# Layer 1 of a fused two-layer block: the chosen prototype weights are split and turned by DMA together with the weighed products, not on TensorE

## The chip, the cores and the metric

The kernel runs on one core of a Trainium2 chip. The metric is device time in microseconds of one execution, lower is better. Before the change three runs gave 3023.6 to 3030.8 us, with a median of 3023.89 us.

A core has TensorE (PE; its weight loads are listed as PEld), VectorE (DVE), ScalarE (ACT), GpSimd (POOL) and SyncE (SP), which here issues nearly all DMAs. Each has a queue of its own, works through it in order, and waits on semaphores.

## The reference, cut to what matters

Two layers work on `x` (64 sequences of 256 rows, 256 wide). Each adds a gated cross-attention over 77 context rows and then a gated feed-forward part. The part in question is the feed-forward of layer 1: each row chooses its two nearest of 32 prototypes and passes through their low-rank matrices, with weights that sum to 1.

```python
d2 = x2 + p2[None, :] - 2.0 * (xf @ prototypes.T)
dists = jnp.sqrt(jnp.maximum(d2, 0.0))
w = jax.nn.softmax(-dists / t, axis=1)
topw, topi = jax.lax.top_k(w, 2)
topw = topw / jnp.sum(topw, axis=1, keepdims=True)
for tslot in range(2):
    idx = topi[:, tslot]
    wt = topw[:, tslot:tslot + 1]
    h = jnp.einsum('nri,ni->nr', B[idx], xf)            # rank 16
    y = jnp.einsum('nor,nr->no', A[idx], h) + bias[idx]
    out = out + wt * y
x = x + jnp.tanh(g_ffn[1]) * out
```

The kernel computes all 32 x 16 = 512 low products of a row (`low`), multiplies them by the row's weights (`wsel`, 32 numbers, two of them not zero) and multiplies the result `hw` by the stacked up-matrices. The bias of the chosen prototypes is one more product, of `wsel` with the 32 x 256 table of biases.

## The kernel before

**Stages.** First come the keys and values and layer 0 (to about 1460 us of the profile). From there to the end runs `attention_ffn_phase`, layer 1, which the change touches. Its unit is a tile of 128 rows, 128 tiles in all. A body is one sequence, that is two tiles, h = 0 and h = 1. Bodies 0 to 15 and 48 to the end are written out, and bodies 16 to 47 are a loop of 16 bodies that runs twice.

**Pipeline.** A body works on many tiles at once: the scores of tile t, its softmax sums one tile later, its normalising two later, its turned probabilities and the product with the values three later (`attend`, L1465), the second layer norm (4), the low products (5), the choice of prototypes (6), the weighing (7), the up-product and the store (8). Nothing schedules this. The order of the code in each engine's `body` is the order in its queue, and semaphores tie the queues together.

**Exact products.** TensorE works on float16 pairs: a number is written as a high half and a low half, and `matmul3` (L150 to L152) adds hi x hi, hi x lo and lo x hi. The high half is always written by ACT with a copy; the low half is the difference from the original, on POOL or DVE.

**The weighed products.** `hw` (128 x 512) is made on POOL (`weigh`, L1199). ACT writes its high half (`weighed_high`, L1336) and POOL its low half (`weighed_low`, L1178) into `hw_parts`. A DMA transpose from SP (`turn_weighed`, L1095) turns the 1024 columns into `hwT`, eight blocks of 128 x 128. A tile later TensorE multiplies them by the up-matrices (12 products).

**The chosen weights.** DVE makes two rows of picks (L1658, two instructions a tile) and adds them into `wsel` (L1665). It writes the sum three times side by side, 96 columns, since the bias product wants hi, hi and lo rows. TensorE transposes `wsel` (L1502) into a PSUM bank, ACT copies 96 rows of it as float16 (`wselT`, L1384), and DVE subtracts to make the low half of the last 32 rows (L1638). The product of `wselT` with the three-part bias table (L1486) closes the up-product.

**Banks.** Five PSUM banks go round in a fixed order of uses (`Ring`). In a body the uses are, for h = 0: probT 0, probT 1, probT 2, ffn, low 0, low 1, wselT, out, q 0, q 1; for h = 1: probT 0, q 2, probT 1, probT 2, ffn, low 0, low 1, wselT, q 3, out. Each use waits until the use five places earlier has been read. So in h = 0 low 1 waits until DVE has read probT 0 (the first `a_probT_lo`, L1527), and `out` (attend) needs all three.

**POOL's order in a tile** (L1211 and on): in h = 0 first the low half of the normed rows (`rows_low`, L1168, one a body); then weigh (L1199), normalise (L1160, two pieces), the low half of `hw` (L1178), the choice's arithmetic (L1186 to L1192), the low half of the normed tile (L1173), and the softmax sums in three steps (L1148, L1150, L1151). A wait stands between the three steps, none between L1151 and the L1168 that follows it.

**DVE's order around the picks**: residual (L1604), statistics (L1645), weight (L1592, L1597: 128 x 1, two SBUF inputs), two picks (L1658), `wsel` (L1665), nearest prototypes (L1574, L1579), and with the next tile the row sums (L1539, L1541), three `a_probT_lo` (L1527) and the maxima.

Of the kernel before, what the change touches and what calls it, by code (L numbers as in the profile page):

```python
# [83 lines left out]
class Ring:  # L84
# [624 lines left out]
def attention_ffn_phase(nc, ctx, psum, const, src, src_rows, dst, keys, values, wq, score_scale, ffn, experts):  # L709
# [267 lines left out]
    def uses(i):  # L977

        names = []
        for h in range(TPB):  # L980
# [8 lines left out]
            names += of(7, [("wselT", h)])  # L989
# [6 lines left out]
    ring = Ring(uses, WORK, 0, END, BODIES)  # L996

    def freed(i, use):
# [11 lines left out]
        return (wselT_ready, t - 6) if what == "wselT" else (out_ready, t - 7)  # L1010
# [34 lines left out]
    def _(sp):  # L1045
# [45 lines left out]
        def turn_weighed(t, p):  # L1091
# [3 lines left out]
            sp.dma_start_transpose(hwT[p][:, :, :], flat(hw_parts[:, :, :])).then_inc(hwT_in[p], 16)  # L1095
# [41 lines left out]
    def _(pool):  # L1137
        pool.memset(wsel[:, :], 0.0).then_inc(wsel_zero, 1)
# [55 lines left out]
        def weigh(t, h):  # L1194
# [6 lines left out]
                               wsel[:, 0:NPROTO].unsqueeze(2).broadcast_to([P, NPROTO, RANK]), ALU.mult)\  # L1201
# [196 lines left out]
    def _(pe):  # L1398
# [67 lines left out]
        def body(i, u, j):  # L1466
            for h in range(TPB):
# [9 lines left out]
                if live(t - 8, NT):  # L1477
# [3 lines left out]
                    need(pe, wselT_ready, t - 7)  # L1481
# [4 lines left out]
                    filled(nc.tensor.matmul(bank[:, 0:D], wselT[:, :], ffn["bias"][:, :], start=False, stop=True),  # L1486
# [12 lines left out]
                if live(t - 7, NT):  # L1499
# [13 lines left out]
    def _(dve):  # L1513
# [94 lines left out]
        def body(i, u, j):  # L1608
            for h in range(TPB):
# [25 lines left out]
                if live(t - 7, NT):  # L1635
# [1393 lines left out]
```

## Time and profile before

| | before |
|---|---|
| median of three runs | 3023.89 us (3023.6 to 3030.8) |
| profiled execution | 3015.37 us |
| its span | 3013.7 us |
| PE busy | 2738.8 us (91%) |
| DVE busy | 2461.3 us (82%) |
| ACT busy | 2199.1 us (73%) |
| POOL busy | 2084.7 us (69%) |
| mean granted TensorE clock | 0.971 of full speed |

The profile is of one execution. Times in it are microseconds from the start of its span. The granted clock is full in all of layer 1 but its start, its end and some microseconds at 2205, where the loop ends one turn and begins the next. A body of layer 1 takes about 23.3 us in the loop and 23.15 us behind it.

### The profile page before, as it was taken

Reading aid. Unit: us, or ns where it says so; the run is one execution under the profiler, and the core shown is the slowest. Engines: PE = TensorE matmul, PEld = TensorE weight load, DVE = VectorE, ACT = ScalarE, POOL = GpSimd, SP = SyncE. Lnnn points to the kernel's source line nnn. Section 1 sums busy time; section 2 is a strip of 40 time slices with the busy share of each in tenths; the row PEclk is TensorE's granted clock in tenths of the full one; section 3 lists DMA queues with packets and bytes.
Section 4 is the critical chain, followed back from the end, with each engine's and each line's share of the span. In section 5 each row is a group of like instructions: output and inputs, shape, how many; then the busy total and the mean of one; then the engine's idle time right before and its main releaser. Section 6 shows DMA issues by size and latency. Waiting matters only on the chain.

```text
span 3013.7 us, 96194 instructions
## 1 busy us (share of the span) xinstructions
PE 2738.8 (91%) x31534; PEld 2164.9 (72%) x31534; DVE 2461.3 (82%) x5870; ACT 2199.1 (73%) x5452; POOL 2084.7 (69%) x2777
## 2 busy tenths in 40 slices
PE   3889897899999999789799999999999999999996
PEld 2444444687778777657588888888888888888884
DVE  6787786688888888675589989888888888989884
ACT  2666666677777777575577777788877788778873
POOL 3893000576667666644378888888888888888886
PEclk7999999899999999999899999999999999999998
DMA  5997666223223223632467777677776777767763
GB/s 153 354 352 293 242 256 255 78 78 92 84 80 89 83 81 94 221 101 59 103 144 162 151 152 149 145 152 149 149 142 147 150 151 146 149 149 153 148 132 79
DMA packets 568793, 455.47 MB, mean 151 GB/s; under 512 B 383616, under 2 KB 527600, under 8 KB 555312
## 3 DMA queue, kind: packets, MB, share of 16 engines
q1 hardware_dynamic: 548144, 402.29, 53.2%
q0 software_dynamic: 7328, 23.40, 2.5%
q10 hardware_dynamic: 12960, 25.23, 2.3%
q8 instruction: 195, 3.19, 0.5%
q14 instruction: 166, 1.36, 0.2%
HBM read 235.08 MB, written 148.83 MB: 127 GB/s over the span
## 4 chain that ended last, share of the span: by engine, by line
PE 33%; DVE 10%; issue 4%; POOL 2%; DMA 1%; ACT 1%; SPq 0%; DVEq 0%; POOLq 0%; ACTq 0%
PE banks L150 10%; PE banks L152 9%; PE banks L151 9%; DVE a_pick L1658 2%; PE banks L1450 2%; DVE a_probT_lo L1527 2%; PE banks L1436 2%; DVE a_y L1604 1%; DVE a_rsum L1539 1%; DVE a_stats L1645 1%; DVE a_wtop L1597 1%; PE banks L1502 0%; DVE a_qT_lo L1525 0%; DVE a_smax L1546 0%; POOL a_pn L1160 0%
## 5 line engine op out<-in xcount | busy, mean ns | idle before, releaser
L383 POOL TENSOR_TENSOR a_probT_lo<-a_expT,a_probT_hi 128x512 f16<-128x512 f32 x256 | 291.5, 1160 | 218.4 <-ACT a_probT_hi L466 218.4
L459 ACT ACTIVATE a_expT<-banks,a_top,w_score_scale 128x512 f32<-128x512 f32 (+1 forms) x384 | 272.3, 709 | 152.4 <-PE banks L550 146.0
L1160 POOL TENSOR_TENSOR a_pn<-a_prob,a_rsum 128x1024 f32<-128x1024 f32 (+1 forms) x256 | 310.3, 1233 | 53.3 <-DVE a_rsum L1541 53.2
L1243 ACT ACTIVATE a_qT_hi<-banks 128x512 f16<-128x512 f32 x252 | 149.8, 595 | 210.1 <-PE banks L152 210.1
L150 PE MATMUL banks<-a_xnT,w_q_hi 128*128 128x256 f16 x1024 | 281.9, 275 | 15.8 <-DMA a_xnT<-a_xn_parts 13.9
L150 PE MATMUL banks<-a_vo_front,a_probT_hi 128*128 128x256 f16 x1024 | 279.5, 273 | 9.6 <-DVE a_probT_lo L1527 3.6
L151 PE MATMUL banks<-a_xnT,w_q_hi 128*128 128x256 f16 x1024 | 281.7, 275 | 0.0
L152 PE MATMUL banks<-a_xnT,w_q_lo 128*128 128x256 f16 x1024 | 281.5, 275 | 0.0
L152 PE MATMUL banks<-a_vo_front,a_probT_lo 128*128 128x256 f16 x1024 | 279.3, 273 | 0.0
L151 PE MATMUL banks<-a_vo_front,a_probT_hi 128*128 128x256 f16 x1024 | 279.3, 273 | 0.0
L1243 ACT ACTIVATE a_probT_hi<-banks 128x512 f16<-128x512 f32 (+1 forms) x384 | 193.8, 517 | 42.2 <-PE banks L1450 41.3
L1525 DVE TENSOR_TENSOR a_qT_lo<-banks,a_qT_hi 128x512 f16<-128x512 f32 x252 | 172.3, 684 | 45.5 <-ACT a_qT_hi L1243 40.7
L550 PE MATMUL banks<-ident,a_shifted 128*128 128x128 f32 (+1 forms) x1280 | 204.4, 284 | 5.3
L1527 DVE SCALAR_TENSOR_TENSOR a_probT_lo<-banks,a_probT_hi 128x512 f16<-128x512 f32 (+1 forms) x384 | 206.9, 581 | 0.3 <-ACT a_probT_hi L1243 0.3
L2397 DVE SCALAR_TENSOR_TENSOR kv_vo_out<-banks,kv_vo_out 128x512 f16<-128x512 f32 (+1 forms) x312 | 191.6, 679 | 16.5 <-ACT kv_vo_out L2295 16.5
L1450 PE MATMUL banks<-ident,a_pn 128*128 128x128 f32 (+1 forms) x1280 | 197.6, 278 | 2.0 <-issue 2.0
L659 DVE TENSOR_TENSOR a_shifted<-banks,a_smax 128x1024 f32<-128x1024 f32 (+1 forms) x256 | 192.2, 793 | 3.8
L2295 ACT ACTIVATE kv_vo_out<-banks 128x512 f16<-128x512 f32 (+1 forms) x312 | 172.4, 603 | 29.4 <-DMA vo<-kv_vo_out 22.1
L150 PE MATMUL banks<-w_downT_hi,a_ynT 128*128 128x288 f16 (+1 forms) x512 | 145.0, 283 | 47.5 <-DVE a_probT_lo L1527 45.1
L1199 POOL TENSOR_TENSOR a_hw<-a_low,a_wsel 128x512 f32<-128x512 f32 x128 | 135.4, 1058 | 72.7 <-DVE a_wsel L1665 72.7
L649 DVE TENSOR_REDUCE a_smax<-banks 128x16 f32<-128x1232 f32 x128 | 183.6, 1435 | 2.2 <-PE banks L536 1.9
L1278 ACT ACTIVATE a_prob<-banks,a_third_shift,w_score_scale 128x77 f32<-128x77 f32 x512 | 170.7, 414 | 12.0 <-ACT a_third_shift L1273 0.4
(383 smaller groups left out, 10315.9 us busy)
## 6 DMA issues: line engine op xcount, KB each, us to landing
vo<-kv_vo_out SPq DMA_DIRECT2D x38, 2048.0 KB, 7.8
a_vo_front<-vo SPq DMA_DIRECT2D x128, 512.0 KB
kt<-kv_k_out ACTq DMA_DIRECT2D x9, 2560.0 KB, 15.0
a_k<-kt SPq DMA_DIRECT2D x64, 308.0 KB, 3.4
kv_raw_e<-in_L_ffn_w POOLq DMA_DIRECT2D x16, 1024.0 KB, 8.8
a_x<-in_x SPq DMA_DIRECT2D x64, 256.0 KB, 2.9
a_y<-in_x SPq DMA_DIRECT2D x64, 256.0 KB, 2.7
x<-a_y SPq DMA_DIRECT2D x64, 256.0 KB, 2.8
```

The lines of the kernel that those rows point to most:

```text
L150: nc.tensor.matmul(out, lhs[0], rhs[0], start=start, stop=False)
L151: nc.tensor.matmul(out, lhs[0], rhs[1], start=False, stop=False)
L152: return nc.tensor.matmul(out, lhs[1], rhs[0], start=False, stop=stop)
L383: pool.tensor_tensor(probT[b][1][:, first:end, :], expT[b][:, first:end, :], probT[b][0][:, first:end, :], ALU.subtract).then_inc(prob_rea ...
L459: act.activation(expT[1 - h][0:rows, first:end, :], bank, ACT.Exp, bias=top[0:rows, 0:1], scale=weights["score_scale"][0:rows, 0:1]).then_ ...
L550: last = nc.tensor.transpose(bank[0:rows, c * P:(c + 1) * P], shifted[1 - h][:, place:place + rows], ident[:, :])
L659: last = nc.vector.tensor_tensor(shifted[h][:, cols].rearrange("p (r h k) -> p r h k", r=TILES, k=end - first), held_scores[:, :, :, first ...
L1160: last = pool.tensor_tensor(keys_of(pn[h]), e[:, :, first:end].rearrange("p (a c) k -> p a c k", a=outer), rsum[h][:, :].rearrange("p (a c ...
L1243: act.activation(out, bank[:, 0:cols].rearrange("p (c s) -> p c s", c=out.shape[1]), ACT.Copy, scale=scale)\
L1450: last = nc.tensor.transpose(bank[0:rows, c * P:(c + 1) * P], turned, ident[:, :])
L1527: nc.vector.scalar_tensor_tensor(out=lo, in0=bank, scalar=scale, in1=hi, op0=ALU.mult, op1=ALU.subtract)\
L2397: nc.vector.scalar_tensor_tensor(out=vo_out[q][0:m, placed(b), 1, :], in0=product_banks(g, c, b, m), scalar=1.0 / OUT_TOP, in1=vo_out[q][0 ...
```

## The change

Into one tile of 1152 columns, `hw_all`, go the 1024 columns of `hw_parts`, the 96 columns of `wsel_parts` (hi, hi, lo) and 32 columns of zeros. `wsel` shrinks to 32 columns.

```diff
-    wsel = sb("wsel", [P, P])
-    wselT = sb("wselT", [BIAS_ROWS, P], F16)
+    wsel = sb("wsel", [P, NPROTO])
-    hw_parts = sb("hw_parts", [P, 2, LOW], F16)
-    hwT = [sb(f"hwT{p}", [P, 2 * LC, P], F16) for p in range(2)]
+    TURNED = 2 * LC + 1
+    hw_all = sb("hw_all", [P, TURNED * P], F16)
+    hw_parts = hw_all[:, 0:2 * LOW].rearrange("p (s n) -> p s n", s=2)
+    wsel_parts = hw_all[:, 2 * LOW:2 * LOW + BIAS_ROWS].rearrange("p (r n) -> p r n", r=3)
+    hwT = [sb(f"hwT{p}", [P, TURNED, P], F16) for p in range(2)]
...
-            names += of(7, [("wselT", h)])
+            names += of(7, [("spare", h)])
...
-            sp.dma_start_transpose(hwT[p][:, :, :], flat(hw_parts[:, :, :])).then_inc(hwT_in[p], 16)
+            sp.dma_start_transpose(hwT[p][:, :, :], hw_all[:, :]).then_inc(hwT_in[p], 16)
...
+        sp.wait_ge(pad_zero, 1)
         load_x(2, 2, 0)
...
-        pool.memset(wsel[:, :], 0.0).then_inc(wsel_zero, 1)
+        pool.memset(hw_all[:, 2 * LOW + BIAS_ROWS:], 0.0).then_inc(pad_zero, 1)
...
             need(pool, hw_hi, t + 1)
+            pool.tensor_tensor(wsel_parts[:, 2, :], wsel[:, :], wsel_parts[:, 0, :], ALU.subtract)
             pool.tensor_tensor(hw_parts[:, 1, :], hw[:, :], hw_parts[:, 0, :], ALU.subtract).then_inc(hw_lo, 1)
...
+            act.activation(wsel_parts[:, 0:2, :], wsel[:, :].unsqueeze(1).broadcast_to([P, 2, NPROTO]), ACT.Copy)
             act.activation(hw_parts[:, 0, :], hw[:, :], ACT.Copy).then_inc(hw_hi, 1)
...
-                    act.activation(wselT[:, :], bank[0:BIAS_ROWS, 0:P], ACT.Copy).then_inc(wselT_hi, 1)
...
-                    need(pe, wselT_ready, t - 7)
...
-                    filled(nc.tensor.matmul(bank[:, 0:D], wselT[:, :], ffn["bias"][:, :], start=False, stop=True),
+                    filled(nc.tensor.matmul(bank[:, 0:D], hwT[turned][0:BIAS_ROWS, 2 * LC, :], ffn["bias"][:, :], start=False, stop=True),
...
-                    need(pe, wsel_ready, t - 6)
-                    bank = bank_for(i, ("wselT", h))
-                    filled(nc.tensor.transpose(bank[:, 0:P], wsel[:, :], ident[:, :]), i, ("wselT", h))
...
-                    nc.vector.tensor_tensor(wselT[rows, :], bank[rows, 0:P], wselT[rows, :], ALU.subtract)\
-                        .then_inc(wselT_ready, 1)
...
-                    need(dve, wselT_ready, t - 6)
-                    need(dve, hw_ready, t - 6)
-                    nc.vector.tensor_tensor(wsel[:, 0:BIAS_ROWS].rearrange("p (r n) -> p r n", r=3),
...
+                    need(dve, hw_lo, t - 6)
+                    nc.vector.tensor_tensor(wsel[:, :], pick[:, 0, :], pick[:, 1, :], ALU.add).then_inc(wsel_ready, 1)
```

The ring keeps an unused place, called `spare`, where `wselT` stood, so that no other use moves to another bank. Nobody fills or waits for it; the waits look one round further back. A bank now has its own number of fills in a body, so that the loop bodies hold some more register instructions on DVE and ACT.

Three places in the order of instructions, all in a late body, h = 1 first on POOL, which now splits the chosen weights ahead of the weighed products (`a_hw_all` is the new joint tile, `a_hw_parts` the old one). Before:

```order
L1199 TENSOR_TENSOR a_hw<-a_low,a_wsel 128x512
L1160 TENSOR_TENSOR a_pn<-a_prob,a_rsum 128x2x8x64
L1160 TENSOR_TENSOR a_pn<-a_prob,a_rsum 128x8x2x13
L1178 TENSOR_TENSOR a_hw_parts<-a_hw,a_hw_parts 128x512
L1186 TENSOR_TENSOR a_dist<-a_square,a_numbers 128x2
```

and now:

```order
L1208 TENSOR_TENSOR a_hw<-a_low,a_wsel 128x512
L1168 TENSOR_TENSOR a_pn<-a_prob,a_rsum 128x2x8x64
L1168 TENSOR_TENSOR a_pn<-a_prob,a_rsum 128x8x2x13
L1186 TENSOR_TENSOR a_hw_all<-a_wsel,a_hw_all 128x32
L1187 TENSOR_TENSOR a_hw_all<-a_hw,a_hw_all 128x512
L1195 TENSOR_TENSOR a_dist<-a_square,a_numbers 128x2
```

POOL has one instruction more in each tile. On ACT a copy moves from behind the low products to ahead of the high half of `hw`. Before:

```order
L1305 ACTIVATE a_inv<-a_rstd 128x1
L1336 ACTIVATE a_hw_parts<-a_hw 128x512
L1370 ACTIVATE a_yn<-a_y,a_shift,a_rstd 128x256
L1311 ACTIVATE a_ysq<-a_inv,a_mv 128x1
L1328 ACTIVATE a_yn_parts<-a_yn 128x256
L1381 ACTIVATE a_low<-banks 128x256 x2
L1384 ACTIVATE a_wselT<-banks 96x128
```

and now:

```order
L1314 ACTIVATE a_inv<-a_rstd 128x1
L1345 ACTIVATE a_hw_all<-a_wsel 128x64
L1346 ACTIVATE a_hw_all<-a_hw 128x512
L1380 ACTIVATE a_yn<-a_y,a_shift,a_rstd 128x256
L1320 ACTIVATE a_ysq<-a_inv,a_mv 128x1
L1337 ACTIVATE a_yn_parts<-a_yn 128x256
L1391 ACTIVATE a_low<-banks 128x256 x2
```

ACT has as many instructions as before. On TensorE the transpose between the low products and `attend` is gone. Before:

```order
L151 MATMUL banks<-w_downT_lo,a_ynT 128x256
L152 MATMUL banks<-w_downT_hi,a_ynT 128x256
L1502 MATMUL banks<-ident,a_wsel 128x128
L150 MATMUL banks<-a_vo_front,a_probT_hi 128x256
L151 MATMUL banks<-a_vo_front,a_probT_hi 128x256
```

and now:

```order
L157 MATMUL banks<-w_downT_lo,a_ynT 128x256
L158 MATMUL banks<-w_downT_hi,a_ynT 128x256
L156 MATMUL banks<-a_vo_front,a_probT_hi 128x256
L157 MATMUL banks<-a_vo_front,a_probT_hi 128x256
```

The bias product itself stays. DVE loses the subtraction for `wselT` (L1638).

## Rows read from the trace of the kernel before

**Rows 1.** Busy time by engine in the loop's stretch (windows; us and instructions).

```profile
1860.00:2580.00 720.00, 693.48 (x8464) 601.80 (x8463) 633.83 (x1810) 572.26 (x1719) 630.16 (x894) 1.00 0.72 148
```

**Rows 2.** What PE waited for, 1500 to 3000: total us, times, longest.

```profile
PE banks L150 <- DVE a_probT_lo L1527: 48.9, 63, 1.8
PE banks L150 <- DMA a_hwT<-a_hw_parts: 12.1, 5, 5.5
```

**Rows 3.** Timeline of DVE around one turn of a body: start, us, instruction, [idle before].

```profile
2696.68 0.48 DVE L1604 SCALAR_TENSOR_TENSOR a_y<-banks,out_scale,a_y 128x256 f32<-128x256 f32 x1 [1.39 <-PE banks L152]
...
2697.86 0.13 DVE L1597 TENSOR_TENSOR a_wtop<-a_late,a_wtop 128x1 f32<-128x1 f32 x1
2698.03 1.71 DVE L1658 TENSOR_SCALAR a_pick<-iota,a_topf,a_wtop 128x32 f32<-128x32 f32 x2
2699.77 0.26 DVE L1665 TENSOR_TENSOR a_wsel<-a_pick 128x96 f32<-128x96 f32 x1
...
2700.97 1.55 DVE L1527 SCALAR_TENSOR_TENSOR a_probT_lo<-banks,a_probT_hi 128x512 f16<-128x512 f32 x3
```

**Rows 4.** Timeline of POOL in the half body before and at that turn.

```profile
2691.93 1.16 POOL L1178 TENSOR_TENSOR a_hw_parts<-a_hw,a_hw_parts 128x512 f16<-128x512 f32 x1 [0.24 <-ACT a_hw_parts L1336]
...
2697.16 0.73 POOL L1150 TENSOR_TENSOR a_quarter<-a_half 128x256 f32<-128x256 f32 x1
2697.97 0.61 POOL L1151 TENSOR_TENSOR a_quarter<-a_quarter,a_prob 128x208 f32<-128x208 f32 x1
2698.54 1.16 POOL L1168 TENSOR_TENSOR a_xn_parts<-a_xn,a_xn_parts 128x512 f16<-128x512 f32 x1
2700.11 1.06 POOL L1199 TENSOR_TENSOR a_hw<-a_low,a_wsel 128x512 f32<-128x512 f32 x1 [0.41 <-DVE a_wsel L1665]
```

**Rows 5.** Chain that ended last, by line (page, whole span).

```profile
PE banks L150 10%; PE banks L152 9%; PE banks L151 9%; DVE a_pick L1658 2%; PE banks L1450 2%; DVE a_probT_lo L1527 2%; PE banks L1436 2%; DVE a_y L1604 1%; DVE a_rsum L1539 1%; DVE a_stats L1645 1%; DVE a_wtop L1597 1%; PE banks L1502 0%; DVE a_qT_lo L1525 0%; DVE a_smax L1546 0%; POOL a_pn L1160 0%
```

**Rows 6.** Timeline of ACT in h = 1 of the same body.

```profile
2689.16 0.38 ACT L1243 ACTIVATE a_probT_hi<-banks 104x256 f16<-104x256 f32 x1 [0.44 <-PE banks L1450]
...
2691.15 0.19 ACT L1305 ACTIVATE a_inv<-a_rstd 128x1 f32<-128x1 f32 x1
2691.24 0.62 ACT L1336 ACTIVATE a_hw_parts<-a_hw 128x512 f16<-128x512 f32 x1
```

**Rows 7.** Chain in order of time, same stretch: start, us on the chain, instruction.

```profile
2691.94 0.11 PE banks L1502
...
2700.97 0.64 DVE a_probT_lo L1527
2701.65 0.28 PE banks L150
...
2702.48 0.16 PE banks L1502
```

**Rows 8.** POOL's small and middle operations, whole run: ns min/median/max.

```profile
L1173 POOL TENSOR_TENSOR a_yn_parts<-a_yn,a_yn_parts x128: 667/670/675, 1506.5 to 2985.4; 128x256 f16<-128x256 f32 x128
...
L1186 POOL TENSOR_TENSOR a_dist<-a_square,a_numbers x128: 188/196/206, 1526.8 to 2996.9; 128x2 f32<-128x2 f32 x128
```

**Rows 9.** Timelines of DVE and POOL in body 8, where experts are added.

```profile
1663.35 1.31 DVE L1658 TENSOR_SCALAR a_pick<-iota,a_topf,a_wtop 128x32 f32<-128x32 f32 x2
...
1663.25 1.16 POOL L1168 TENSOR_TENSOR a_xn_parts<-a_xn,a_xn_parts 128x512 f16<-128x512 f32 x1
```

**Rows 10.** Timelines of DVE and POOL in an early h = 0.

```profile
1554.65 1.00 DVE L1658 TENSOR_SCALAR a_pick<-iota,a_topf,a_wtop 128x32 f32<-128x32 f32 x2
...
1554.68 0.73 POOL L1150 TENSOR_TENSOR a_quarter<-a_half 128x256 f32<-128x256 f32 x1
```

**Rows 11.** Landing of the hwT transpose (whole run), and its first reader in one body.

```profile
DMA to landing us min/median/max: 3.0/3.1/6.3
...
2698.72 0.27 PE L150 MATMUL banks<-w_upT_hi,a_hwT 128*128 128x256 f16 x1
```

**Rows 12.** The chain from 2915 us to the end, by line.

```profile
by line: issue 14.8%; POOL a_pn L1160 8.4%; POOL a_hw_parts L1178 8.0%; POOL a_hw L1199 7.5%; DMA a_hwT<-a_hw_parts 6.1%; POOL a_half L1148 5.1%; PE banks L150 4.8%; PE banks L152 4.4%; PE banks L151 4.2%; POOL a_dist L1189 4.1%; POOL a_lat
```

More of the change, by code:

```diff
@@ L84, with __init__ @@
 class Ring:
-    def __init__(self, uses, banks, first, last, steady):
-        self.banks, self.steady = banks, steady
+    def __init__(self, uses, banks, first, last, steady, spare=None):
+        self.banks, self.steady, self.spare = banks, steady, spare
         self.flat, self.at_use = [], {}
+        filled = [0] * banks
         for i in range(first, last):
             for name in uses(i):
-                self.at_use[i, name] = len(self.flat)
+                filled[len(self.flat) % banks] += name[0] != spare
+                self.at_use[i, name] = len(self.flat), filled[len(self.flat) % banks]
                 self.flat.append((i, name))
-        self.per = len(uses(steady))
-        assert self.per % banks == 0
+        kept = uses(steady)
+        assert len(kept) % banks == 0
+        start = self.at_use[steady, kept[0]][0]
+        self.per = [sum(name[0] != spare for name in kept[(s - start) % banks::banks]) for s in range(banks)]
         tails = [uses(i)[-banks:] for i in (steady - 1, steady)]
@@ L100, in fill @@
     def fill(self, i, name):
-        n = self.at_use[i if isinstance(i, int) else self.steady, name]
-        k = n // self.banks + 1
-        return n % self.banks, k if isinstance(i, int) else (i - self.steady) * (self.per // self.banks) + k
+        n, k = self.at_use[i if isinstance(i, int) else self.steady, name]
+        s = n % self.banks
+        return s, k if isinstance(i, int) else (i - self.steady) * self.per[s] + k
     def before(self, i, name):
-        n = self.at_use[i if isinstance(i, int) else self.steady, name] - self.banks
+        n = self.at_use[i if isinstance(i, int) else self.steady, name][0] - self.banks
+        while n >= 0 and self.flat[n][1][0] == self.spare:
+            n -= self.banks
         if n < 0:
@@ L799, in attention_ffn_phase @@
         sem("top_step"), sem("wtops_ready"), sem("picked"), sem("wsel_ready"))
-    low_ready, hw_ready, hw_hi, hw_lo, wselT_hi, wselT_ready, out_ready = (
-        sem("low_ready"), sem("hw_ready"), sem("hw_hi"), sem("hw_lo"), sem("wselT_hi"), sem("wselT_ready"),
-        sem("out_ready"))
+    low_ready, hw_ready, hw_hi, hw_lo, out_ready = (
+        sem("low_ready"), sem("hw_ready"), sem("hw_hi"), sem("hw_lo"), sem("out_ready"))
     minus_made = sem("minus_made")
@@ L1009, in freed @@
             return y_ready, t - 2
-        return (wselT_ready, t - 6) if what == "wselT" else (out_ready, t - 7)
+        return out_ready, t - 7
     def bodies(eng, body):
@@ L1200, in weigh @@
                                low[h][:, :].rearrange("p (n r) -> p n r", n=NPROTO),
-                               wsel[:, 0:NPROTO].unsqueeze(2).broadcast_to([P, NPROTO, RANK]), ALU.mult)\
+                               wsel[:, :].unsqueeze(2).broadcast_to([P, NPROTO, RANK]), ALU.mult)\
                 .then_inc(hw_ready, 1)
@@ L1381, in body @@
                         act.activation(low[1 - h][:, part], bank[:, 0:LOW // LU], ACT.Copy).then_inc(low_ready, 1)
-                if live(t - 7, NT):
-                    bank = full(i, ("wselT", h))
-                    act.activation(wselT[:, :], bank[0:BIAS_ROWS, 0:P], ACT.Copy).then_inc(wselT_hi, 1)
                 prep(4)
@@ L1634, in body @@
                     prototype_products(i, t - 5, h)
-                if live(t - 7, NT):
-                    bank, rows = full(i, ("wselT", h)), slice(2 * NPROTO, BIAS_ROWS)
-                    need(dve, wselT_hi, t - 6)
-                    nc.vector.tensor_tensor(wselT[rows, :], bank[rows, 0:P], wselT[rows, :], ALU.subtract)\
-                        .then_inc(wselT_ready, 1)
                 prep(4)
```

10 lines of the change are left out of this document (2 added, 8 removed).

## The prediction, made before the changed kernel was run

> **What bounds the kernel now.** I read the busy time first, then PE's waits, then the chain, then one turn of a body on each engine. Only layer 1 is touched, from about 1460 us on. In the loop's stretch of 720 us PE is busy 693.5, 96% [rows 1], so it looks like a kernel that TensorE bounds. But PE stands still about once a body, 48.9 us in 63 waits, and always for DVE's first `a_probT_lo` [rows 2]: low 1 needs the bank that it frees. So a loop through DVE sets the pace.
>
> Follow it back. `a_probT_lo` runs at 2700.97, behind the picks and `wsel` on DVE [rows 3]. The residual before them starts at 2696.68, as soon as PE has given it, and the last small weight (L1597) ends at 2697.99. Yet the two picks, 128 x 32 each, last 1.71 us, from 2698.03 to 2699.74, where `wsel` with 96 columns lasts 0.26; two like that would take 0.5 [rows 3]. POOL shows why: L1151 ends at 2698.58 and L1168 at 2699.70 [rows 4], and the second pick is done 0.04 us behind the latter. A pick that comes while POOL works is held until POOL's instruction ends, and since nothing stands between L1151 and L1168, the second pick is held for L1168 too. The chain charges 2% of the span, some 60 us, to L1658 [rows 5], about 1 us for each of 60 bodies.
>
> The Trainium skill (SBUF — State Buffer, "Who interferes with whom") has the reason: VectorE and GpSimd share one port pair, which `tensor_scalar` in its two-port mode holds exclusively, and the other fully blocks. By that rule, the trace agrees: both picks end with a POOL instruction.
>
> So what matters is when POOL ends L1168. POOL's queue is full back to L1178 at 2691.93, which waited 0.24 us for ACT [rows 4]. ACT's queue is full back to 2689.16, where it waited for PE's last turned probabilities in h = 1 [rows 6]. The loop is: PE turns probabilities in h = 1, ACT up to the high half of `hw` (ends 2691.86), POOL up to L1168 (2699.70), DVE up to `a_probT_lo` (2701.61), PE low 1 at 2701.65 [rows 7], `attend` of h = 0, and without a gap on to the next turning. PE's own way from that turning to the residual at 2696.68 reaches the picks 1.2 us too early: 2698.03 + 0.5 = 2698.5 for two picks that nothing holds, against 2699.74. Work taken from PE there is worth nothing; work put on ACT ahead of L1336 or on POOL between L1178 and L1168 is paid in full.
>
> **The change part by part**, per body, h = 1 unless said.
>
> ACT: the copy of 64 columns goes ahead of L1336, which is on the loop. A 128 x 1 lasts 0.19 and a 128 x 512 0.62 [rows 6], so 64 columns last about 0.19 + 0.43 x 63/511 = 0.24. The next instruction starts 0.10 before the end (2691.15 + 0.19 against 2691.24), so it costs 0.14; I take **+0.15**. Bounds: 0.09 (the step of the 128 x 1) and 0.52 (that of the 512). The copy L1384 that goes stood behind it and off the loop: nothing gained.
>
> POOL: the new 128 x 32 subtraction. A 128 x 2 lasts 0.196 and a 128 x 256 0.670 [rows 8]; between them 32 columns give 0.25. Neighbours overlap by 0.04 (2698.58 against 2698.54), so **+0.20**. Bounds 0.14 and 0.63. The 0.24 us that POOL waits before L1178 covers none of it, since the wait is for ACT and the new instruction waits for the same signal.
>
> DVE: `wsel` falls from 96 to 32 columns, between 0.26 [rows 3] and the 0.13 of a 128 x 1, about 0.17: **-0.09** on the loop, bounds 0 and -0.13. The subtraction L1638 goes, but DVE waits for PE anyway (1.39 us before L1604 [rows 3]): nothing. The new wait on `hw_lo` before `wsel` looks late: `hw_lo` of the tile before is signalled at 2691.93 + 1.16 = 2693.09, plus 0.35, and `wsel` runs at 2699.77. Over 6 us in hand; behind it in the queue would be row sums and `a_probT_lo`.
>
> PE, h = 0: the transpose took 0.16 of the chain at 2702.48 [rows 7], between low 1 and `attend`. But `attend` needs the third `a_probT_lo`, which ends at 2700.97 + 1.55 = 2702.52 [rows 3], and PE starts 0.04 after a release (2701.61 to 2701.65). So it may begin at 2702.56 to 2702.58 instead of 2702.64: **-0.06**, bounds 0 and -0.16.
>
> PE, h = 1: the transpose takes 0.11 [rows 7]. It only brings the residual 0.11 earlier to picks that are held: **0**, as above; -0.11 if the hold were gone.
>
> Sum: 0.15 + 0.20 - 0.09 - 0.06 = **+0.20 us a body**.
>
> Does the hold stay? POOL comes 0.35 later and DVE 0.11 earlier. L1150 then runs 2697.51 to 2698.24, and L1597 arrives at 2697.75: held until L1150 ends. The first pick comes 0.04 later, at 2698.28, and L1151 starts 0.08 after L1150 as now, at 2698.32. The trace has that very case: pick at 1554.65, POOL at 1554.68, and 1.00 us for the picks [rows 10], so a pick that comes 0.03 ahead is held all the same. It waits out L1151, and the second pick waits out L1168, to 2700.09. The pattern at the end is today's.
>
> That goes for some 46 bodies: +9.2 us. In the first dozen the experts are added and DVE runs later: the picks start at 1663.35, when L1168 (1663.25) already runs, so the first is held and the second ends 0.25 after L1168 (1664.66 against 1664.41) [rows 9]. With the shift of 0.46 it becomes the late pattern, which ends 0.04 behind L1168: 0.2 back, and nothing in sum.
>
> Tail: from 2915 us POOL leads the chain. 8.0% of 98.7 us are L1178 [rows 12], seven at 1.13 us each: 7 x 0.20 = 1.4. hwT has 6.1%, two landings of 3.0 us. The transpose carries nine blocks for eight; by size 3.1/8 = 0.39 at most and 0 at least, I take 0.17: 0.3. With ACT's 0.15 three times and `wsel`'s 0.09 three times back: **+1.9**. Start: SP waits for the memset before its first load, 0.1 us.
>
> DMA: hwT starts after 2693.1, lands 3.1 later, 2696.3, and is read at 2698.72 [rows 11]: 2.4 us in hand, 1.8 after the change. PE waited for it five times [rows 2]. Nothing.
>
> Total: 9.2 + 0 + 1.9 + 0.1 = +11.2. The profiled execution took 3015.4 (span 3013.7 and 1.7 around it): 3026.6. The median of the runs lies 8.5 above it, 3023.9: **3035**.
>
> **The rivals.**
>
> *PE bounds after all* (faster). For it: 96% busy, and every PE instruction but one wait a body on the chain. Then a body saves 0.11 + 0.06 + 0.09 = 0.26, over 60 bodies 15.6 us: 3009 or so. Against it: the end of the picks 0.04 behind L1168.
>
> *The picks slip into a gap* (faster). If ACT and POOL together cost over 0.55, L1150 starts after L1597 has passed; the first pick waits out L1150 only, the second takes the 0.08 us gap before L1151, and `wsel` waits out L1151 but not L1168. DVE would be 0.6 us earlier, and PE's wait of 0.77 a body (48.9/63) nearly goes: 46 x 0.65 = 30 us, about 2996. My terms give 0.35, their upper bounds more.
>
> *Who comes first gets the port.* The same section of the skill says that whoever issues first gets the pair. By that rule the pick at 2698.28 would go ahead of L1151 at 2698.32. Worked out from rows: the second pick waits out L1151 to 2698.97, and `wsel`, with two SBUF inputs, waits out L1168 to 2700.05 and ends 0.1 later, at 2700.16, where I expect 2700.09 + 0.17 = 2700.28 after the picks. That gives 0.1 a body back, +6 us in all: 3030. The early case speaks against it [rows 10].
>
> *The nine-block transpose is slow* (slower). Eight is a power of two and nine is not, and the trace shows no such transpose. At twice the landing (6.3, the row's maximum) hwT would come at 2699.9 for 2698.6, and `ynT` behind it later still, about 1 us a body: +60, 3085. Against it: the two sizes of transpose in use both work.
>
> *It comes out even*: ACT's and POOL's terms at their lower ends (0.23) against DVE's and PE's at their upper ones (0.29): 3024 to 3027.
>
> **How the numbers follow.** Below 0.3%, 9 us, a measurement can't tell a change from none. Forecast 0.54: its own range is +0.08 to +0.38 a body, 3029 to 3044; 0.44 of it is slower by more than 0.3%, 0.10 within. PE 0.12, gap 0.12, port rule 0.08, slow transpose 0.06, even 0.08. Faster 0.24, same 0.26, slower 0.50. The range leaves out the gap and the slow transpose: 3006 to 3046.
>
> **What would show it.** Right: PE's wait for `a_probT_lo` grows from 48.9 to about 70 us (0.20 + 0.11 + 0.05 more a body); the copy steps 0.15 and the subtraction 0.20; the picks still end 0.04 behind L1168 (now L1176); a body takes 23.35 late and 23.5 in the loop. Wrong: picks that end before L1168 does, a wait that shrinks, or PE waiting for hwT in mid-phase.

## The result, and the profile after

| | before | after |
|---|---|---|
| median of seven runs | 3023.60 us (3021.69 to 3030.80) | 3038.46 us (3035.11 to 3042.17) |
| ratio to before | | 1.0047, 95% interval 1.0035 to 1.0059 |
| profiled execution, its span | 3015.37, 3013.7 us | 3037.44, 3035.0 us |
| a body in the loop / behind it | 23.30 / 23.14 us | 23.64 / 23.45 us |

The change makes the kernel 0.47% slower, 14.9 us; the forecast was 3035 us, 11.2 us more. A body is read from one h = 0 residual to the next in DVE's timeline; the table has means.

The busy time in the loop's stretch, as in [rows 1]:

```profile
1860.00:2580.00 720.00, 675.84 (x8291) 583.68 (x8284) 621.75 (x1729) 567.50 (x1700) 636.43 (x938) 1.00 0.72 149
```

PE is busy 17.6 us less, DVE 12.1 less and ACT 4.8 less. POOL is busy 6.3 more, and the kernel is slower. The same 720 us now hold fewer bodies (23.64 us each for 23.30), so a part of each fall is only the slower pace: worked out per body, PE has 0.25 us less, DVE 0.10 less, ACT 0.11 more and POOL 0.50 more. What PE waited for in layer 1 (total us, times, longest) answers to [rows 2]:

```profile
PE banks L156 <- DVE a_probT_lo L1528: 77.4, 124, 1.8
PE banks L156 <- DMA a_ynT<-a_yn_parts: 6.5, 9, 2.0
PE banks L156 <- DMA a_hwT<-a_hw_all: 5.0, 4, 2.3
```

The wait for `a_probT_lo` has grown by 28.5 us and comes twice a body where it came once. DVE's timeline at the turn of a body behind the loop (start, us, instruction, [idle before]) answers to [rows 3]; its last row is the next body's residual:

```profile
2712.26 0.48 DVE L1605 SCALAR_TENSOR_TENSOR a_y<-banks,out_scale,a_y 128x256 f32<-128x256 f32 x1 [1.29 <-PE banks L158]
...
2713.43 0.54 DVE L1598 TENSOR_TENSOR a_wtop<-a_late,a_wtop 128x1 f32<-128x1 f32 x1
2714.01 1.80 DVE L1654 TENSOR_SCALAR a_pick<-iota,a_topf,a_wtop 128x32 f32<-128x32 f32 x2
2715.84 0.19 DVE L1660 TENSOR_TENSOR a_wsel<-a_pick 128x32 f32<-128x32 f32 x1
...
2716.97 1.55 DVE L1528 SCALAR_TENSOR_TENSOR a_probT_lo<-banks,a_probT_hi 128x512 f16<-128x512 f32 x3
...
2735.71 0.48 DVE L1605 SCALAR_TENSOR_TENSOR a_y<-banks,out_scale,a_y 128x256 f32<-128x256 f32 x1 [1.30 <-PE banks L158]
```

And POOL's, which answers to [rows 4]:

```profile
2707.77 0.25 POOL L1186 TENSOR_TENSOR a_hw_all<-a_wsel,a_hw_all 128x32 f16<-128x32 f32 x1 [0.65 <-ACT a_hw_all L1346]
2707.98 1.16 POOL L1187 TENSOR_TENSOR a_hw_all<-a_hw,a_hw_all 128x512 f16<-128x512 f32 x1
...
2713.22 0.74 POOL L1158 TENSOR_TENSOR a_quarter<-a_half 128x256 f32<-128x256 f32 x1
2714.03 0.61 POOL L1159 TENSOR_TENSOR a_quarter<-a_quarter,a_prob 128x208 f32<-128x208 f32 x1
2714.61 1.16 POOL L1176 TENSOR_TENSOR a_xn_parts<-a_xn,a_xn_parts 128x512 f16<-128x512 f32 x1
2716.11 1.06 POOL L1208 TENSOR_TENSOR a_hw<-a_low,a_wsel 128x512 f32<-128x512 f32 x1 [0.34 <-DVE a_wsel L1660]
```

The picture is that of before, moved. The body takes 2735.71 - 2712.26 = 23.45. L1598 ends at 2713.97, 0.01 behind L1158 (2713.96), where L1597 was held by nothing at the turn of [rows 3]; the prediction had that. The picks start 0.02 ahead of L1159 and end at 2715.81, 0.04 behind L1176 (2715.77). ACT's timeline in h = 1 answers to [rows 6]:

```profile
2704.85 0.39 ACT L1252 ACTIVATE a_probT_hi<-banks 104x256 f16<-104x256 f32 x1 [0.44 <-PE banks L1457]
...
2706.84 0.19 ACT L1314 ACTIVATE a_inv<-a_rstd 128x1 f32<-128x1 f32 x1
2706.93 0.25 ACT L1345 ACTIVATE a_hw_all<-a_wsel 128x64 f16<-128x64 f32 x1
2707.07 0.62 ACT L1346 ACTIVATE a_hw_all<-a_hw 128x512 f16<-128x512 f32 x1
```

The last fence of after is PE at that turn; it shows where the second wait of a body is:

```profile
2715.60 0.28 PE L1492 MATMUL banks<-w_low_bias,a_hwT 96*128 96x256 f16 x1
2716.36 0.30 PE L156 MATMUL banks<-w_downT_hi,a_ynT 128*128 128x288 f16 x1 [0.48 <-DMA a_ynT<-a_yn_parts]
...
2717.66 0.28 PE L156 MATMUL banks<-w_downT_hi,a_ynT 128*128 128x256 f16 x1 [0.39 <-DVE a_probT_lo L1528]
...
2718.67 0.27 PE L156 MATMUL banks<-a_vo_front,a_probT_hi 128*128 128x256 f16 x1 [0.19 <-DVE a_probT_lo L1528]
```

### The profile page after: what moved, and what is told of

It is laid out like the page before. It is cut to its first block, busy times and chain, and to the rows that moved or that the text cites. A ratio compares the mean times of both kernels' runs of the same rounds, so it can differ in the third digit from the quotient of the medians.

```text
span 3035.0 us, 95761 instructions
## 1 busy us (share of the span) xinstructions
PE 2724.8 (90%) x31406; PEld 2148.6 (71%) x31406; DVE 2442.4 (80%) x5742; ACT 2201.6 (73%) x5452; POOL 2114.3 (70%) x2905
## 4 chain that ended last, share of the span: by engine, by line
PE 34%; DVE 9%; issue 5%; POOL 2%; DMA 1%; ACT 1%; DVEq 0%; SPq 0%; POOLq 0%; ACTq 0%
PE banks L156 10%; PE banks L158 10%; PE banks L157 10%; PE banks L1457 2%; DVE a_pick L1654 2%; PE banks L1443 2%; DVE a_probT_lo L1528 2%; DVE a_wtop L1598 1%; DVE a_y L1605 1%; DVE a_stats L1641 1%; DVE a_rsum L1540 1%; POOL a_hw_all L1187 0%; POOL a_pn L1168 0%; DVEq L62 0%; DVE a_topi L1580 0%
## 5 line engine op out<-in xcount | busy, mean ns | idle before, releaser
L1168 POOL TENSOR_TENSOR a_pn<-a_prob,a_rsum 128x1024 f32<-128x1024 f32 (+1 forms) x256 | 310.6, 1235 | 51.7 <-DVE a_rsum L1542 51.5
L1156 POOL TENSOR_TENSOR a_half<-a_prob 128x512 f32<-128x512 f32 x128 | 166.5, 1301 | 14.1 <-ACT a_prob L1363 14.0
```

Source lines behind the costliest of these rows:

```text
L1168: last = pool.tensor_tensor(keys_of(pn[h]), e[:, :, first:end].rearrange("p (a c) k -> p a c k", a=outer), rsum[h][:, :].rearrange("p (a c ...
```

## Experiments

All were compared with the kernel before on the same chip. Bodies are means in us: the first dozen (read from bodies 3 to 12), the loop, behind it. Ratios have their 95% intervals.

| kernel | median, us | ratio to before | dozen | loop | behind |
|---|---|---|---|---|---|
| before | | 1 | 23.98 | 23.30 | 23.14 |
| after | 3038.46 | 1.0047 (1.0035 to 1.0059) | 23.95 | 23.64 | 23.45 |
| e1_swap | 3020.87 | 1.0016 (1.0002 to 1.0030) | 23.84 | 23.47 | 23.28 |
| e2_hidden | 3009.58 | 0.9981 (0.9969 to 0.9993) | 23.68 | 23.26 | 23.10 |
| e4_pool_op | 3027.24 | 1.0039 (1.0028 to 1.0051) | 23.90 | 23.51 | 23.35 |
| e6_nine_blocks | 3016.56 | 0.9999 (0.9989 to 1.0010) | 23.97 | 23.31 | 23.15 |
| e7_removed_only | 3012.49 | 0.9986 (0.9975 to 0.9996) | 23.92 | 23.26 | 23.12 |
| e11_even_after | 3036.01 | 1.0055 (1.0041 to 1.0069) | 23.93 | 23.65 | 23.45 |
| e3_rows_later | 3004.89 | 0.9957 (0.9940 to 0.9974) | 23.49 | 23.12 | 23.05 |
| e12_removed_rows_later | 3002.02 | 0.9956 (0.9942 to 0.9970) | 23.44 | 23.14 | 23.04 |
| e13_pool_op_rows_later | 3015.86 | 0.9994 (0.9984 to 1.0004) | 23.64 | 23.24 | 23.32 |
| e8_after_rows_later | 3019.19 | 1.0012 (1.0002 to 1.0021) | 23.54 | 23.48 | 23.13 |
| e9_hidden_rows_later | 3012.31 | 0.9990 (0.9978 to 1.0002) | 23.55 | 23.41 | 23.01 |
| e10_even_hidden_later | 3017.66 | 0.9987 (0.9977 to 0.9997) | 23.53 | 23.45 | 23.04 |

Medians are from different chips; compare the ratios.

### Where the additions stand

**e1_swap**: the weighed products first on both engines, the chosen weights behind them.

```diff
-            pool.tensor_tensor(wsel_parts[:, 2, :], wsel[:, :], wsel_parts[:, 0, :], ALU.subtract)
-            pool.tensor_tensor(hw_parts[:, 1, :], hw[:, :], hw_parts[:, 0, :], ALU.subtract).then_inc(hw_lo, 1)
+            pool.tensor_tensor(hw_parts[:, 1, :], hw[:, :], hw_parts[:, 0, :], ALU.subtract)
+            need(pool, wsel_hi, t + 1)
+            pool.tensor_tensor(wsel_parts[:, 2, :], wsel[:, :], wsel_parts[:, 0, :], ALU.subtract).then_inc(hw_lo, 1)
...
-            act.activation(wsel_parts[:, 0:2, :], wsel[:, :].unsqueeze(1).broadcast_to([P, 2, NPROTO]), ACT.Copy)
             act.activation(hw_parts[:, 0, :], hw[:, :], ACT.Copy).then_inc(hw_hi, 1)
+            act.activation(wsel_parts[:, 0:2, :], wsel[:, :].unsqueeze(1).broadcast_to([P, 2, NPROTO]), ACT.Copy)\
+                .then_inc(wsel_hi, 1)
```

> The changed kernel, with the order turned round on two engines: ACT copies hw first and the chosen weights behind it, POOL subtracts for hw first (on the signal of hw alone) and for the chosen weights behind it. Theory (the loop goes through ACT's high half of hw and POOL up to rows_low, with the picks held): ACT's 0.15 us leaves the loop, POOL's 0.20 stays in it, so a late body takes 23.30 us, against 23.45 in the changed kernel and 23.15 before; about 3031 us. Rival (the loss comes from something else that the change brings, the longer transpose or the register instructions): the body stays at 23.45 and the time at 3038.

A late body takes 23.28 (expected 23.30), and the ratio is 1.0016, where the expected 3031 us would be 1.0025, within the interval. ACT's copy was on the loop.

**e2_hidden**: both additions in a gap of their queue. `chosen_high` is ACT's copy with a signal of its own (`wsel_hi`); it now stands ahead of the third `a_probT_hi`.

```diff
+            need(pool, wsel_hi, t + 1)
+            pool.tensor_tensor(wsel_parts[:, 2, :], wsel[:, :], wsel_parts[:, 0, :], ALU.subtract)
             need(pool, hw_hi, t + 1)
-            pool.tensor_tensor(wsel_parts[:, 2, :], wsel[:, :], wsel_parts[:, 0, :], ALU.subtract)
             pool.tensor_tensor(hw_parts[:, 1, :], hw[:, :], hw_parts[:, 0, :], ALU.subtract).then_inc(hw_lo, 1)
...
+                    if g == PG - 1 and live(t - 7, NT):
+                        chosen_high(t - 7, u, h, j)
                     if live(t - 3, NT):
                         split_hi(i, ("probT", h, g), ...
```

> The changed kernel, with both additions put where their engines wait anyway: ACT's copy of the chosen weights ahead of the last turned probabilities (0.44 us idle there), POOL's subtraction ahead of its wait for the high half of hw (0.24 us idle). Theory: nothing is added to the loop, the shorter wsel takes 0.065 off it, a late body takes 23.09 to 23.12 us and PE waits for a_probT_lo 0.75 us in each; 3020 to 3025 us, level with before or a little below. Rival (transpose or registers): 23.45 and 3038, as in the changed kernel. Rival (PE bounds, its work was saved): 0.2 or more below before, 22.9 a body, 3010.

In e2 a stretch of ACT, then of POOL, from their timelines:

```profile
2685.74 0.25 ACT L1354 ACTIVATE a_hw_all<-a_wsel 128x64 f16<-128x64 f32 x1
2686.30 0.38 ACT L1253 ACTIVATE a_probT_hi<-banks 104x256 f16<-104x256 f32 x1 [0.30 <-PE banks L1468]
...
2688.37 0.62 ACT L1346 ACTIVATE a_hw_all<-a_hw 128x512 f16<-128x512 f32 x1
...
2688.52 0.24 POOL L1186 TENSOR_TENSOR a_hw_all<-a_wsel,a_hw_all 128x32 f16<-128x32 f32 x1
2689.06 1.16 POOL L1188 TENSOR_TENSOR a_hw_all<-a_hw,a_hw_all 128x512 f16<-128x512 f32 x1 [0.30 <-ACT a_hw_all L1346]
```

ACT waits 0.30 for PE where it waited 0.44, so the copy lies in that wait; POOL still waits 0.30 for ACT behind its subtraction. From ACT's last probabilities to the high half of `hw` it is 2.07 us, in the changed kernel 2.22 (2704.85 to 2707.07): ACT's 0.15 is gone. Behind the loop a body takes 23.10, as expected (23.09 to 23.12), and bodies 3 to 12 gain 0.30 each, which I had not worked out; so the ratio, 0.9981, is a little below the 0.9988 to 1.0005 of the expected times. The same work, moved, makes the kernel 0.66% faster than after (0.9981 by 1.0047) and a little faster than before. In e1 only the copy leaves the path, and a body is 0.17 shorter than in after. The place costs, not the work.

**e4_pool_op**: before, with one 128 x 32 subtraction more on POOL ahead of L1178.

```diff
+            pool.tensor_tensor(unused[:, :], hw[:, 0:NPROTO], hw_parts[:, 0, 0:NPROTO], ALU.subtract)
             pool.tensor_tensor(hw_parts[:, 1, :], hw[:, :], hw_parts[:, 0, :], ALU.subtract)
```

> The kernel before, with one more 128 x 32 subtraction on POOL behind its wait for the high half of hw, into a tile that nobody reads. Theory: 0.20 to 0.22 us more in each body, 23.36 late, and the picks end 0.04 behind rows_low as before; 3034 us. Rival (POOL's idle 0.24 us takes it up, or POOL is not on the loop): 23.15 and 3024.

Its two rows in POOL's timeline:

```profile
2721.95 0.24 POOL L1179 TENSOR_TENSOR a_unused<-a_hw,a_hw_parts 128x32 f16<-128x32 f32 x1 [0.45 <-ACT a_hw_parts L1338]
2722.15 1.16 POOL L1180 TENSOR_TENSOR a_hw_parts<-a_hw,a_hw_parts 128x512 f16<-128x512 f32 x1
```

A step of 0.20, and 0.21 more a body in the loop and behind it (expected 0.20 to 0.22): paid in full, although POOL waits 0.45 for ACT right ahead of it.

### What was removed, the transpose, the registers

**e7_removed_only**: after without its copy and its subtraction and with eight blocks turned; the bias product reads zeros, so the chosen biases are left out.

```diff
-            act.activation(wsel_parts[:, 0:2, :], wsel[:, :].unsqueeze(1).broadcast_to([P, 2, NPROTO]), ACT.Copy)
...
-            pool.tensor_tensor(wsel_parts[:, 2, :], wsel[:, :], wsel_parts[:, 0, :], ALU.subtract)
```

> The removals alone: TensorE's transpose, ACT's copy and DVE's subtraction are gone and wsel has 32 columns, but nothing is added to ACT, POOL or the DMA. The biases of the chosen prototypes are left out of the result (that product reads zeros). Theory: only wsel's 0.065 us is on the loop, a late body takes 23.08 us, low 1 to attend stays at 1.015 us although the transpose between them is gone, PE's wait grows by 0.05 to 0.1 a body; about 3020 us. Rival (PE's work counts): 0.26 less a body, 22.9, and 3008 us.

The rival in which PE bounds falls here: the means are 23.26 and 23.12, only 0.04 and 0.02 shorter, where that rival wanted 0.26 less a body. The median body behind the loop is 23.08, as expected, and low 1 to `attend` still takes 1.015. PE is rid of two transposes and waits the time away (stretch of layer 1):

```profile
PE banks L156 <- DVE a_probT_lo L1528: 58.5, 117, 1.7
```

That is 9.6 us more than before [rows 2].

**e6_nine_blocks**: before, turning nine blocks, the ninth all zeros.

```diff
...
-            sp.dma_start_transpose(hwT[p][:, :, :], flat(hw_parts[:, :, :]))
+            sp.dma_start_transpose(hwT[p][:, :, :], hw_all[:, :])
```

> The kernel before, with hwT's transpose alone enlarged from eight to nine blocks (the ninth holds zeros and nobody reads it); the chosen weights go their old way over TensorE. Theory: 23.15 us a late body as before, the transpose lands in 3.3 us for 3.1, PE waits for hwT only at the end; 3024 to 3026 us. Rival (the longer transpose costs part of the 15 us): PE waits for hwT or ynT in mid-phase, 0.1 us or more a body, 3029 or above.

Landing of that transpose, from issue, in e6:

```profile
DMA to landing us min/median/max: 3.2/3.4/5.9
```

It lands 0.3 later than with eight blocks [rows 11], and the time does not move.

**e11_even_after**: after, but the unused place of the ring counts as a fill, so that the loop has no more register instructions than before.

```diff
-                filled[len(self.flat) % banks] += name[0] != spare
+                filled[len(self.flat) % banks] += 1
...
+                            if n == LU - 1 and c == 0 and ("spare", h) in uses(i if isinstance(i, int) else BODIES):
+                                filled(last, i, ("spare", h))
                         filled(last, i, ("low", h, n))
```

> The changed kernel with the even count of fills alone, so without the extra register instructions in the loop. Theory (DVE's picks are held until POOL's L1176 ends, so that what DVE does ahead of them is free): no change, 23.61 us a body in the loop and 23.45 behind it, ratio to before 1.0047. Rival (the register instructions are part of what the change costs in the loop): the loop falls by 0.1 to 0.3 a body, 3 to 9 us in all.

Nothing moves: 23.65 and 23.45. The interval of the ratio (1.0041 to 1.0069) holds the expected 1.0047.

### The hold by `rows_low` taken away

**e3_rows_later**: before, with `rows_low` behind `weigh` in POOL's order. Nothing is added or removed.

```diff
-                if h == 0 and live(i + 1, NB):
-                    rows_low(i + 1)
                 if live(t - 7, NT):
                     weigh(t - 7, 1 - h)
+                if h == 0 and live(i + 1, NB):
+                    rows_low(i + 1)
```

> The kernel before, with POOL's rows_low (128 x 512, L1168) moved from ahead of weigh to behind it, so that in h = 1 to h = 0 nothing follows the last softmax sum but a wait for wsel. Theory (the picks are held by POOL's instructions): the second pick ends 0.04 us behind the last softmax sum and not behind rows_low, wsel comes about 1.1 us earlier, PE's wait of 0.77 us a body goes nearly or wholly, and PE's work or POOL's (21.3 us a body) bounds next: 22.3 to 22.8 us a body, 2980 to 3005 us. Rival (the picks are long for a reason of their own, POOL is a bystander): the picks still last 1.7 us, the body stays at 23.15 or grows, since xnT is turned later.

DVE, then POOL, at a turn of e3:

```profile
2689.55 0.45 DVE L1597 TENSOR_TENSOR a_wtop<-a_late,a_wtop 128x1 f32<-128x1 f32 x1
2690.04 0.51 DVE L1658 TENSOR_SCALAR a_pick<-iota,a_topf,a_wtop 128x32 f32<-128x32 f32 x2
2690.59 0.26 DVE L1665 TENSOR_TENSOR a_wsel<-a_pick 128x96 f32<-128x96 f32 x1
...
2689.38 0.61 POOL L1151 TENSOR_TENSOR a_quarter<-a_quarter,a_prob 128x208 f32<-128x208 f32 x1
2690.92 1.06 POOL L1199 TENSOR_TENSOR a_hw<-a_low,a_wsel 128x512 f32<-128x512 f32 x1 [0.93 <-DVE a_wsel L1665]
2691.94 1.16 POOL L1168 TENSOR_TENSOR a_xn_parts<-a_xn,a_xn_parts 128x512 f16<-128x512 f32 x1
```

The two picks take 0.51 where they took 1.71 [rows 3]. This shows the hold by L1168: same instructions, and only POOL's order is another. The hold by L1151 stays. At this turn it is L1597 that lasts 0.45 and ends at 2690.00, 0.01 behind L1151. In bodies 16 to 59 L1151 holds L1597 in 22 and the first pick in the other 22, so the second pick ends 0.56 or 0.24 behind L1151, not 0.04 as I expected. I also expected 22.3 to 22.8 a body, and it is 23.05 to 23.12; the ratio is 0.9957, where 2980 to 3005 us would be 0.986 to 0.994. What binds next, by PE's waits in layer 1 of e3:

```profile
PE banks L150 <- DMA a_hwT<-a_hw_parts: 27.4, 14, 5.5
PE banks L150 <- DMA a_xnT<-a_xn_parts: 14.6, 22, 1.2
PE banks L150 <- DVE a_probT_lo L1527: 9.5, 13, 1.8
```

and by the chain from 2685 to 2709 us, by line:

```profile
by line: issue 24.0%; POOL a_pn L1160 11.1%; POOL a_hw_parts L1178 9.5%; POOL a_dist L1189 8.4%; POOL a_late L1191 7.0%; POOL a_half L1148 5.3%; POOL a_xn_parts L1168 4.7%; POOL a_hw L1199 4.4%; DVE a_wtop L1597 3.9%; POOL a_quarter L1150 3
```

The wait for `a_probT_lo` has nearly gone, and PE now waits for two turned tiles, `hwT` and `xnT`, whose low halves POOL writes. In this stretch POOL's queue leads the chain, and POOL stands 0.93 us before `weigh`, which it did 0.41 before [rows 4].

**e8_after_rows_later** and **e9_hidden_rows_later**: the same move in after and in e2.

> The changed kernel, with rows_low behind weigh as in the run of that name on the kernel before. Theory: the hold by rows_low goes here too, and what the change takes from PE counts from then on, unless POOL (0.4 us more a body) bounds: 22.3 to 22.9 us a body, 2980 to 3010 us, well below both kernels. Rival: as the changed kernel, 3038.

> The changed kernel with both additions where ACT and POOL wait, and rows_low behind weigh. Theory: the shortest of all; with the loop through POOL broken, PE bounds, and its 0.22 us of transposes saved makes a body 0.1 to 0.3 us shorter than the kernel before with rows_low behind weigh: 22.1 to 22.6 us, 2970 to 2995 us. Rival (POOL's queue bounds next): level with that kernel or above it.

Both missed: their ratios stay above e3's by 0.55 and 0.33 percentage points, so that the rival of e9's text (level with e3 or above it) came. e9's body behind the loop is as short as e3's, but in its loop it takes 23.41 against 23.12. **e10_even_hidden_later** tried my first reason, that the extra register instructions come to light once DVE is not held: e9 with the even count of e11.

> The kernel with both additions in the gaps and rows_low behind weigh, and one thing more: the unused place in the ring counts as a fill (a product of low 1 signals it), so that every bank has four fills in a body as before, and the loop bodies of DVE and ACT are rid of the extra register instructions (413 to 381 in DVE's code, 281 to 249 in ACT's). Without it the loop took 23.3 to 23.4 us a body against 22.94 behind the loop, where before with rows_low later took 22.77 to 23.1 in the loop and 22.97 behind it; its chain shows issue pieces of 0.4 to 0.56 us on DVE ahead of the picks and of a_qT_lo, where the other has 0.15. Theory (once the hold by L1168 is gone, DVE's register instructions stand on the path): the loop falls to 22.95 to 23.05 a body, 30 bodies x 0.35 = 10 us less, about 2999 to 3003, ratio to before 0.995 to 0.996. Rival (the extra POOL subtraction makes xnT late, and register instructions are hidden): nothing changes, 3010 to 3013, loop 23.3 to 23.4.

That reason fell: e10 takes 23.45 in the loop, so its rival came. The next pair asks which half of the change costs there: **e12_removed_rows_later** is e7 with the move (the chosen biases left out again), **e13_pool_op_rows_later** is e4 with the move.

> The changed kernel without its two additions (the bias product reads zeros, so the chosen prototypes' biases are left out; eight blocks are turned), with rows_low behind weigh. The loop took 22.77 to 23.1 us a body in before with rows_low later, but 23.3 to 23.4 in the three kernels that have it with the change in (copy and subtraction in their places or in the gaps, fills uneven or even). Theory (POOL's own 0.2 us a tile is what the loop cannot hide there: rows_low and with it xnT come later, PE waits for xnT 4 to 6 us in 280): without the additions the loop falls to 22.6 to 22.9 a body and 22.7 behind it, ratio to before 0.990 to 0.994. Rival (what was removed, the transposes on PE and the use of their bank, is what costs there): the loop stays at 23.3, ratio 0.998.

> The kernel before with one more 128 x 32 subtraction on POOL a tile, ahead of hw_lo (its result is not used), and rows_low behind weigh. Theory (POOL's 0.2 us a tile is what the loop cannot hide): the loop takes 23.2 to 23.5 a body where it takes 22.77 to 23.1 without the subtraction, ratio to before 0.999 to 1.002. Rival (the removals cost it): as before with rows_low later, 0.9957.

With the removals alone the move gives what it gives before (0.9956 and 0.9957), so they neither help nor harm there within the intervals, and the 0.990 to 0.994 that I hoped for did not come. One POOL subtraction of 0.25 us brings the ratio from 0.9957 to 0.9994, about 11 us, as expected (0.999 to 1.002). So POOL's time is paid without the hold by L1168 too. But the picks are not free of POOL there, by e13's timelines of DVE and of POOL (its L1152 is L1151 of before):

```profile
2758.80 0.26 DVE L1599 TENSOR_TENSOR a_wtop<-a_late,a_wtop 128x1 f32<-128x1 f32 x1
2759.10 0.88 DVE L1660 TENSOR_SCALAR a_pick<-iota,a_topf,a_wtop 128x32 f32<-128x32 f32 x2
...
2759.12 0.61 POOL L1152 TENSOR_TENSOR a_quarter<-a_quarter,a_prob 128x208 f32<-128x208 f32 x1
```

In bodies 16 to 59 that softmax sum holds the first pick 42 times of 44, and as often or once more in e8, e9 and e10; in e12 it is 34 times, in e3 22. How much of the 11 us comes by this hold and how much by POOL's own queue is not separated. And e13's loop takes 23.24, e9's 23.41 with the subtraction in a gap. What costs the other 0.17 in e9's loop is open.

## Why the prediction was right, point by point

**What bounds.** Right. The loop through ACT, POOL, the held picks and `a_probT_lo` sets the pace: e3 shows the hold by L1168, e7 that PE does not bound, e1 and e2 that ACT's time counts, e4 that POOL's is paid in full. The picks end 0.04 behind L1176, as forecast.

The Trainium skill (SBUF — State Buffer, "Who interferes with whom") says that issue order decides who blocks. By the trace's start times the first pick starts 0.02 us ahead of L1159 and is held all the same, as in [rows 10], and so it is in all of bodies 16 to 59. So the rival built on that rule fell, though it forecast the body 0.1 shorter only. Whether a start time in the trace tells who issued first, no run here shows.

**The terms of a body**, behind the loop: means of both traces (bodies 48 to 58) between the same two events.

| term | forecast | measured |
|---|---|---|
| ACT's copy (last turned probabilities to high half of `hw`) | +0.15 | +0.153 |
| POOL's subtraction (high half to the start of L1187) | +0.20 | +0.203 |
| L1187 to the end of L1176 | 0 | +0.015 |
| `wsel` with 32 columns (257 to 192 ns) | -0.09 | -0.065 |
| `attend` of h = 0 starts earlier | -0.06 | 0.00 |
| transposes of h = 1 | 0 | 0 |
| sum | +0.20 | +0.306 |
| body | +0.20 | 23.144 to 23.449, +0.305 |

Every other step of the loop is the same within 0.003, among them the 9.64 us from `attend` of h = 0 to ACT's last turned probabilities. Both costs were right to a hundredth. Both gains were mis-sized, 0.06 and 0.025, and they are most of the missing 0.105; the rest is the 0.015 of the third row. The larger is `attend`. From low 1's first product to `attend`'s it takes 1.015 us before and after. The transpose stood there for 0.16 [rows 7], but `attend` waits for the third `a_probT_lo` all the same. That ends at 2716.97 + 1.55 = 2718.52, and PE starts at 2718.67, 0.15 later, where I had put 0.04 to 0.06 from the first one's wake-up. It was so before the change too, and the trace of the kernel before could have told. At the turn of [rows 7] its timelines of PE and of PE's weight loads have

```profile
2702.34 0.30 PE L1502 MATMUL banks<-ident,a_wsel 128*128 128x128 f32 x1
2702.63 0.10 PEld L150 LDWEIGHTS banks<-a_vo_front,a_probT_hi 128*128 128x128 f16 x1 [0.19 <-DVE a_probT_lo L1527]
```

so by these rows `attend`'s first weight load waited for DVE while the transpose was still running. The chain's 0.16 [rows 7] was not a price of the transpose. Its time now shows as the second wait of a body: 63 waits before, 124 now, 0.19 for the second, so about 12 of the 28.5 us that this wait has grown by are the time of the removed transpose turned into a wait. The forecast of 70 us had 0.05 a body for it; 0.19 is more than enough for the 7 us to 77.

**The sum over the phase.** From tile 25's residual to tile 117's, 46 bodies, it is 1076.7 before and 1089.5 after: +12.8, forecast 9.2. In the first dozen bodies (tile 7 to 25) it is 215.29 and 215.26: the forecast 0. There the second pick ended 0.24 behind L1168 and now ends 0.04 behind L1176, as worked out. From tile 117 to the end it is 3.6 more, forecast 1.9 and two or three bodies at 0.3; before, e1, e2, e4 and e6 vary there from 143.4 to 146.6 us, so this is not settled closer. The last 4.9 us of the spans' 21.3 come ahead of tile 7. The first residual came between 1498.6 and 1508.3 us in the traces of all kernels, whose earlier stages are the same, so they are no part of the change, and the medians differ by 14.9 alone. So +14.9 stands against +11.2. In the 46 bodies 0.105 more a body would be 4.8 us; it is 3.6, since the turn of the loop near 2205 is 0.5 us shorter (27.9 to 27.4). That is about the difference of the medians, and the tail's 1.7 more than forecast lie within what single traces differ by. Some luck is in the total: the forecast for the profiled execution was 3026.6, and it took 3037.4, because the forecast put the median 8.5 above it as before, and now it lies 1.0 above it.

**The transposed bias rows.** Right: nine blocks cost nothing (e6). `hwT`'s landing in the changed kernel, against 3.1 [rows 11]:

```profile
DMA to landing us min/median/max: 3.2/3.3/6.0
```

One thing was missed: `ynT` now comes late at the turn shown, where PE waits 0.48 for it and then 0.39 for `a_probT_lo`. Over layer 1 such waits are 9 with 6.5 us, and were 4 with 2.4. I had only looked at `hwT`. At this turn the wait costs nothing extra, since low 1 waits for `a_probT_lo` all the same.

**The rivals.** PE bounds: no (e7). Gap: no, the shift of 0.35 kept the pattern. Who comes first: no, as said above. Slow transpose: no (e6). Even: no, ACT's and POOL's terms came at the values taken, not at their lower ends, and the gains stayed below theirs.

## What to carry to other kernels

Before taking work from the busiest engine, find the loop that sets the pace and put new instructions where their queue waits for something later: here the same change costs 0.47% with its copy and subtraction on that loop, and gains 0.19% with both in gaps (e2). Look at instructions on DVE that last much longer than their size asks for, and see what POOL does then. Moving one POOL instruction behind the wait (e3, 0.43% faster than before, the fastest complete kernel of this study) gained more than the change did even with its additions in gaps. With it, the gaps of e2 no longer paid (e9 stays above e3), so a gap on another engine may not be free a second time.

## What the runs showed of the hardware

- In the changed kernel the second of two 128 x 32 picks on DVE ended 0.04 us behind POOL's L1176, and the two lasted 1.80 us; with `rows_low` moved (e3) they lasted 0.51 at the turn shown.
- A 128 x 1 product of two SBUF operands on DVE is held by POOL like the picks: 0.54 us for L1598 where 0.13 is its length [rows 3], ended 0.01 behind POOL's L1158.
- Small instructions, length and step to the next: ACT 128 x 64 0.25 and 0.14 to 0.15, POOL 128 x 32 0.25 and 0.20 to 0.21, DVE `wsel` 0.26 with 96 columns and 0.19 with 32. Two thirds fewer columns save a quarter.
- PE started 0.15 us behind the end of the third of three DVE instructions and 0.06 behind the first (medians behind the loop, before and after alike; from the rounded rows I had read 0.04 [rows 3, 7]). Why they differ stays open.
- A DMA transpose of nine 128 x 128 float16 blocks landed 3.3 to 3.4 us (median) after its issue, one of eight 3.1 us.
